# Pairs' products put first in each round of a fused DLRM kernel, gathers held behind them, and four table look-ups moved into the rounds

## The reference

```
e = stack([tbl_f[ids[:, f]] for f in range(32)], axis=1)    # 512 x 32 x 256
dots = einsum('bnd,bmd->bnm', e, e)
z = dots[:, i < j]                                          # 512 x 496
h = concatenate([z, dense_ctx], axis=1)                     # 512 x 512
h = maximum(h @ W_top1 + b_top1, 0)                         # 512 x 512
h = maximum(h @ W_top2 + b_top2, 0)                         # 512 x 256
y = h @ W_top3                                              # 512 x 1
```

## Time and profile before

| | |
|---|---|
| time, median of 3 runs | 162.37 us (161.98 to 162.54) |
| span of the profiled execution, first to last instruction | 231.2 us |
| the profiled execution's time beside its span | none is listed |
| TensorE busy, in the profiled execution | 178.4 us (77%) |
| GpSimd busy | 104.5 us (45%) |
| VectorE busy | 95.2 us (41%) |
| ScalarE busy | 77.3 us (33%) |
| mean granted TensorE clock | 0.874 |

### The profile page before, as it was taken

One profiled execution on the slowest core, in us unless ns is written; L12 is line 12 of the kernel. 1 busy time (PEld: TensorE's weight loads), 2 busy tenths in 40 slices (PEclk: granted clock), 3 DMA queues, 4 the chain that ended last, 5 costly groups with the idle time before them and its releaser, 6 DMA issues.

```text
span 231.2 us, 6208 instructions
## 1 busy us (share of the span) xinstructions
PE 178.4 (77%) x2678; PEld 151.4 (66%) x2678; DVE 95.2 (41%) x311; ACT 77.3 (33%) x190; POOL 104.5 (45%) x110
## 2 busy tenths in 40 slices
PE   7999952999958889868494394929559295999995
PEld 6688831688946778757392392819458184899774
DVE  2896310836902859753116014220603232534331
ACT  3376413746843244113032051400304032234232
POOL 2777775565874445372417336360723614300000
PEclk9999995599995999999889559785958769799999
DMA  5999653577883345541303213130220303100000
GB/s 154 311 371 311 172 145 104 171 259 207 256 299 117 122 154 151 184 114 29 91 3 101 80 27 98 41 113 3 71 68 26 106 11 94 45 6 4 4 6 0
DMA packets 12869, 26.77 MB, mean 116 GB/s; under 512 B 2917, under 2 KB 3881, under 8 KB 12842
## 3 DMA queue, kind: packets, MB, share of 16 engines
q0 software_dynamic: 4992, 13.64, 19.9%
q1 hardware_dynamic: 7706, 12.47, 16.5%
q10 hardware_dynamic: 144, 0.26, 0.5%
HBM read 26.36 MB, written 0.00 MB: 114 GB/s over the span
## 4 chain that ended last, share of the span: by engine, by line
PE 65%; issue 21%; ACT 9%; another core or an unknown queue 2%; DVE 1%; POOL 0%; POOLq 0%
PE bank L614 18%; PE bank L565 14%; PE bank L621 13%; PE xt_ps L584 11%; ACT high L450 3%; PE bank L648 3%; ACT kept L458 3%; PE bank L674 2%; ACT xt L463 2%; PE xt_ps L701 2%; PE xt_ps L674 1%; DVE pairs L394 1%; PE bank L682 1%; ACT h L496 0%
## 5 line engine op out<-in xcount | busy, mean ns | idle before, releaser
L346 POOL DMA_INDIRECT rows<-table,row_ids x104 | 103.8, 998 | 94.7 <-PE xt_ps L584 62.1
L614 PE MATMUL bank<-xt 128*32 128x32 f32 (+1 forms) x1664 | 45.2, 219 | 36.9 <-issue 36.0
L614 PEld LDWEIGHTS bank<-xt 128*32 128x32 f32 (+1 forms) x1664 | 35.0, 129 | 47.8 <-issue 44.1
L463 ACT COPY xt<-xt_ps 128x512 f32<-128x512 f32 (+1 forms) x43 | 22.2, 554 | 85.3 <-PE xt_ps L584 75.2
L394 DVE COPY pairs<-bank 32x64 f32<-32x64 f32 (+1 forms) x184 | 39.6, 215 | 12.7 <-PE bank L614 10.4
L377 DVE COPY xt<-xt_ps 128x512 f32<-128x512 f32 (+1 forms) x14 | 9.2, 654 | 84.8 <-PE xt_ps L584 84.8
L584 PE MATMUL xt_ps<-ident,rows 128*128 128x128 f32 x208 | 33.4, 306 | 7.1 <-issue 5.0
L565 PE MATMUL bank<-one_hot,high 128*128 128x512 f32 (+1 forms) x128 | 31.8, 369 | 2.2 <-issue 1.2
L621 PE MATMUL bank<-pairs,w_sb 128*128 128x128 f32 x192 | 32.2, 329 | 1.2 <-issue 1.2
L584 PEld LDWEIGHTS xt_ps<-ident,rows 128*128 128x128 f32 x208 | 26.7, 157 | 9.6 <-issue 5.9
L366 DVE TENSOR_SCALAR one_hot<-small_ids_sb,first_sb 128x512 fp32r<-128x512 int32 (+1 forms) x64 | 24.5, 422 | 17.4 <-remote 11.8
(11 more groups left out here) (36 smaller groups left out, 44.8 us busy)
## 6 DMA issues: line engine op xcount, KB each, us to landing
small_sb<-small_tables SPq DMA_DIRECT2D x31, 256.0 KB
w_sb<-w SPq DMA_DIRECT2D x8, 256.0 KB
rows<-table,row_ids POOLq DMA_INDIRECT x104
small_ids_sb<-small_ids SPq DMA_DIRECT2D x3, 256.0 KB
small_ids_sb<-small_ids SPq DMA_DIRECT2D x4, 128.0 KB
w_sb<-w SPq DMA_DIRECT2D x1, 512.0 KB, 5.6
small_ids_sb<-small_ids ACTq DMA_DIRECT2D x1, 256.0 KB
small_sb<-small_tables SPq DMA_DIRECT2D x2, 128.0 KB, 3.5
```

The source lines that it names most:

```text
L346: nc.gpsimd.indirect_dma_start(rows[:, i % ROWS, :], None, table, bass.IndirectOffsetOnAxis(ap=row_ids[:, i:i + 1], axis=0)).then_inc(gath ...
L463: nc.scalar.copy(*fill_parts(f)).then_inc(xt_act, 1)
L614: done = nc.tensor.matmul(dots_ps[later(n)][n % 2][quads, g, :], x, x, start=(c == 0), stop=(c == DC - 1))
```

## The change

- `AT_ONCE` is 2 for all batches, so a half is always 32 instructions of 64 columns.
- Ahead of the rounds stand twos 0 to 15 (tables 0 to 3) with 8 fills. Twos 16 to 31 (tables 4 to 7) are in rounds 0 to 5, as 2, 2, 2, 2, 4, 4. The fills of the rounds are 4, 3, 3, 3, 3, 4, 4, then 3 each, and 4 in round 14.
- In a round both halves come first, then layers 2 and 3, layer 1, the twos, and the fills.
- take_kept of batches 0 and 1 is behind two 15, and those of 2 to 7 are in rounds 0 to 3.
- A gather that reuses a row buffer waits for more than the transposes: gathers 14 to 20 for the end of two 9 (`chunk_used`), gathers from 21 on for a first half, `dots_half_done`: gathers 21 to 27 for that of batch 0, later ones for the first half of the round after the one in which the buffer was emptied.
- The eight parts of W_top1 and W_top2 are loaded between tables 5 and 6, once fills 7 to 10 (before: 16 to 23) are transposed.

```diff
-AT_ONCE = 2, 1
-FIRST_BATCHES = 6
+AT_ONCE = 2
...
-FILLS_BEHIND = {6: (0, 1, 2), 8: (3, 4, 5), 11: (6, 7, 8), 14: (9, 10, 11), 17: (12, 13), 21: (14, 15), 23: (16,)}
-EARLY = 17
-TWOS_AHEAD = 24
-TWOS_IN = [1, 1, 1, 1, 2, 1, 1]
-KEPT_BEHIND = {17: (0, 1), 20: (2, 3), 23: (4, 5)}
-KEPT_IN = {0: (6,), 1: (7,), 7: (8, 9), 8: (10, 11), 9: (12,), 10: (13,), 11: (14,), 12: (15,)}
-FILLS_IN = [2, 2, 1, 2, 3, 3, 4, 3, 3, 3, 3, 2, 2, 3, 4]
+FILLS_BEHIND = {6: (0, 1, 2), 9: (3, 4, 5), 12: (6, 7)}
+EARLY = 8
+PAUSE_BEHIND = 9
+FILLS_PAUSED = 4
+TWOS_AHEAD = 16
+TWOS_IN = [2, 2, 2, 2, 4, 4, 0]
+KEPT_BEHIND = {15: (0, 1)}
+KEPT_IN = {0: (2, 3), 1: (4, 5), 2: (6,), 3: (7,), 7: (8, 9), 8: (10, 11), 9: (12,), 10: (13,), 11: (14,), 12: (15,)}
+FILLS_IN = [4, 3, 3, 3, 3, 4, 4, 3, 3, 3, 3, 3, 3, 3, 4]
...
-FOUND_BANKS = [(2, 3), (0, 1)] * 3 + [(0, 1)] * 2
-PRODUCTS_FREE = 5
+FOUND_BANKS = [(2, 3), (0, 1)] * 2 + [(0, 1)] * 4
+PRODUCTS_FREE = 3
...
                 if fill_gathers(f)[-1] >= ROWS:
-                    pool.wait_ge(transposed, next(e for e in range(f) if fill_gathers(f)[-1] - ROWS in fill_gathers(e)) + 1)
+                    e = next(e for e in range(f) if fill_gathers(f)[-1] - ROWS in fill_gathers(e))
+                    pool.wait_ge(transposed, e + 1)
+                    if e < FILLS_PAUSED:
+                        pool.wait_ge(chunk_used, 2 * (PAUSE_BEHIND + 1))
+                    else:
+                        pool.wait_ge(dots_half_done, round_of(e) + 2 if e >= EARLY else 1)
...
-                if groups[-1] == GROUPS - 1:
-                    done.then_inc(dots_done, 1)
+                done.then_inc(dots_half_done if h == 0 else dots_done, 1)
...
             for r in range(ROUNDS):
+                dots(2 * r)
+                dots(2 * r + 1)
                 if r in LAYER2_IN:
                     layer2_of(LAYER2_IN[r])
                 if r in LAYER3_IN:
                     layer3(LAYER3_IN[r], l3_ps)
-                if r in LEAD_LAYER1:
-                    b, halves = LEAD_LAYER1[r]
+                if r in LAYER1_IN:
+                    b, halves = LAYER1_IN[r]
                     for i in halves:
                         layer1_half(b, i)
-                dots(2 * r)
-                if r in TRAIL_LAYER1:
-                    b, halves = TRAIL_LAYER1[r]
-                    for i in halves:
-                        layer1_half(b, i)
-                for two in twos_in(r)[:1]:
-                    look_up(two)
-                dots(2 * r + 1)
-                for two in twos_in(r)[1:]:
+                for two in twos_in(r):
                     look_up(two)
```

More of the change, by code:

```diff
@@ L51 @@
 TURNED_BY_ACT = 0, 1, 3
-FILLS_BEHIND = {6: (0, 1, 2), 8: (3, 4, 5), 11: (6, 7, 8), 14: (9, 10, 11), 17: (12, 13), 21: (14, 15), 23: (16,)}
-EARLY = 17
-TWOS_AHEAD = 24
-TWOS_IN = [1, 1, 1, 1, 2, 1, 1]
-KEPT_BEHIND = {17: (0, 1), 20: (2, 3), 23: (4, 5)}
-KEPT_IN = {0: (6,), 1: (7,), 7: (8, 9), 8: (10, 11), 9: (12,), 10: (13,), 11: (14,), 12: (15,)}
-FILLS_IN = [2, 2, 1, 2, 3, 3, 4, 3, 3, 3, 3, 2, 2, 3, 4]
+FILLS_BEHIND = {6: (0, 1, 2), 9: (3, 4, 5), 12: (6, 7)}
[7 more added lines that the diff above has]
+FILLS_IN = [4, 3, 3, 3, 3, 4, 4, 3, 3, 3, 3, 3, 3, 3, 4]
 ROUNDS = len(FILLS_IN)
[L67 to L70, removed]
+LAYER1_IN = {5: (0, [0, 1, 2]), 6: (0, [3, 4, 5]), 7: (0, [6, 7]), 9: (1, [0, 1, 2]), 10: (1, [3, 4, 5]),
+             11: (1, [6, 7]), 13: (2, [0, 1, 2, 3]), 14: (2, [4, 5, 6, 7])}
 RELU1_IN = {7: 0, 11: 1, 14: 2}
@@ L133, in build_tower @@
         banks = [ctx.enter_context(nc.psum_tensor(f"bank{n}", [P, 512], F32)) for n in range(5)]
-        dots_ps = [[bank[:, 0:GROUPS * n * Q].rearrange("p (g j) -> p g j", g=GROUPS) for bank in banks[2:4]]
-                   for n in AT_ONCE]
+        dots_ps = [bank[:, 0:GROUPS * AT_ONCE * Q].rearrange("p (g j) -> p g j", g=GROUPS) for bank in banks[2:4]]
         l1_ps = [[bank[:, n * BLOCK:(n + 1) * BLOCK] for n in range(N1)] for bank in (banks[4], banks[0])]
@@ L169, in build_tower @@
         kept_dve = sem("kept_dve")
+        dots_half_done = sem("dots_half_done")
         dots_done = sem("dots_done")
@@ L254, in fills_in, with round_of @@
             return range(EARLY + sum(FILLS_IN[:r]), EARLY + sum(FILLS_IN[:r + 1]))
-        def later(n):
-            return int(n >= FIRST_BATCHES)
+        def round_of(f):
+            return next(r for r in range(ROUNDS) if f in fills_in(r))
         def moves(n, s):
@@ L265, in moves @@
                 to = pairs[Q * q:Q * (q + 1), b % 2, skip:, at + s * GROUPS:at + (s + 1) * GROUPS]
-                column = s % AT_ONCE[later(n)] * Q + q * JJ
-                source = dots_ps[later(n)][n % 2][Q * s:Q * (s + 1), :, column + skip:column + JJ]
+                column = s % AT_ONCE * Q + q * JJ
+                source = dots_ps[n % 2][Q * s:Q * (s + 1), :, column + skip:column + JJ]
                 yield to, source.rearrange("i g j -> i j g")
@@ L318, in _ @@
                     load_dense(1)
[L319 to L323, removed]
+                if k == 5:
+                    for j in range(JJ):
+                        sp.wait_ge(transposed, EARLY + j // 2)
+                        sp.dma_start(w1_sb[:, j, :], w1[:, j, :]).then_inc(w1_in, 16)
+                    sp.dma_start(w2_sb[:], w2).then_inc(w2_in, 16)
             for b in range(2, NB):
@@ L606, in dots @@
                         pe.wait_ge(moved_dve, n - 1)
-                at_once = AT_ONCE[later(n)]
                 for g in groups:
                     for c in range(DC):
-                        for s in range(0, GROUP, at_once):
+                        for s in range(0, GROUP, AT_ONCE):
                             at = g * GROUP + s
-                            x = xt[:, n % KEEP, c, at:at + at_once, :].rearrange("d s f -> d (s f)")
-                            quads = slice(s * Q, (s + at_once) * Q)
-                            done = nc.tensor.matmul(dots_ps[later(n)][n % 2][quads, g, :], x, x,
+                            x = xt[:, n % KEEP, c, at:at + AT_ONCE, :].rearrange("d s f -> d (s f)")
+                            quads = slice(s * Q, (s + AT_ONCE) * Q)
+                            done = nc.tensor.matmul(dots_ps[n % 2][quads, g, :], x, x,
                                                     start=(c == 0), stop=(c == DC - 1))
-                if groups[-1] == GROUPS - 1:
-                    done.then_inc(dots_done, 1)
+                done.then_inc(dots_half_done if h == 0 else dots_done, 1)
             def layer1(b, n, columns, to):
```

## The result

| | before | after |
|---|---|---|
| time, median (4 runs each) | 162.45 us (161.98 to 162.85) | 180.93 us (180.37 to 181.12) |
| ratio | | 1.112, 95% interval 1.107 to 1.117 |
| span of the profiled execution | 231.2 us | 179.1 us |
| instructions | 6208 | 4977 |

A kernel's executions differ: some are a few per cent longer, at a lower granted clock, and the ratios leave these out while the medians hold them. The lists of the runs hold the span beside the time. The profiled execution after has 180.88 us beside 179.1, and the difference is 1.8 us in all of the lists: that is what lies around the span. So the two spans of the table must not be compared.

What follows compares the result with a forecast made beforehand. The gather stream was taken to set the end from round 8 on. `flip` moves from 137.35 to 150.4, 13.05 us, with 0.78 behind it 13.8; 162.4 + 13.8 = 176.2 us, range 167 to 184.

Steps and rivals of the forecast that it cites:

- Rival C: TensorE is the bound, gathers come closer than 1.25 us, 15.5 us lie around the span: 182.6 us, chance 0.14.
- The gaps as the profiler's doing: Before's profiled execution: 48 us of TensorE issue gaps and the low clock come from profiling, so timed runs lack them.
- Around the span: Time outside before's span: the rebuilt end at 156.3 leaves 6.1 us to the timed median.
- The first hold: Ahead of batch 0: TensorE idles 2.6 us, gather 21 starts at 42.3 instead of 34.1, the stream 8.2 us late.
- Halves: Twenty halves become 64-column: 7.8 us more TensorE work, 0.78 in round 14 and 0.78 in batch 15 on the path.
- Twos in the rounds: Rounds 3 and 4: VectorE's preparations delay fills 18 and 21; TensorE waits 2.8 us in round 3, round 4 repeats it.
- The second hold: Gather 56 waits for dots(12)'s first half, ending at 88.4, against 86.05 by its own pace: 2.4 us.
- W1 comes earlier: Tables 6 and 7 load behind W1's 2.5 MB: zero, or a microsecond or two of round 4.
- B: The first hold alone counts, VectorE's queue is shorter and copies hide: 172.2 us, chance 0.20.
- E: In between, the stream makes up its 8 us through shorter pauses: 163 to 168 us, chance 0.09.
- D: Not slower: gaps before 32-column products are partly real in timed runs and the change removes them; 160.3, chance 0.07.
- A: The likeliest case, the summed terms with the gather stream setting the end: 176.2 us, chance 0.50.

Runs made afterwards that it cites:

- E6: Before with 64-column halves for all batches and gather 56 held until the products of batch 6: 172.23 us, ratio to before 1.061.
- E1: Before with 64-column halves for all batches, nothing else changed: 162.80 us, ratio to before 1.0087.
- E10: E1 with take_kept of batches 0 to 3 behind twos 20 and 22 instead of 17 and 20: 163.67 us, ratio to before 1.0065.
- E11: Before, 32-column halves kept, with take_kept of batches 0 to 3 behind twos 20 and 22 instead of 17 and 20: 164.01 us, ratio to before 1.0071.
- E4: After with 32-column halves from batch 6 on: 185.01 us from four executions of 181.23 to 187.38, too uneven for a ratio.
- E8: After with the added waits of gathers 14 to 27 only, later ones waiting for transposes alone: 175.99 us, ratio to before 1.087.
- E5: E1 with both halves first in each round, layers and twos behind them: 164.39 us, ratio to before 1.017.
- E9: E2 with fills 15, 18 and 21 copied by ScalarE instead of VectorE: 170.83 us, ratio to before 1.044.
- E3: After with W_top1 and W_top2 loaded behind tables 6 and 7: 177.28 us, ratio to before 1.091.
- E12: E2 with W_top1 and W_top2 loaded behind tables 6 and 7, as in E3: 172.53 us, ratio to before 1.062.
- E2: After without the added waits of the gathers, which wait for the transposes alone: 172.04 us, ratio to before 1.065.
- E7: After with the added waits of gathers from 28 on only, 14 to 27 waiting for transposes alone: 175.42 us, ratio to before 1.084.

## Why the prediction was right, point by point

**What bounds the kernel.** Right: the gather stream, at 1.25 us a gather. Shown by E6 (a pause is paid in full), by E1 (7.8 us more of TensorE's work cost 1.4) and E10 (1.4 us won ahead of the rounds were gone at once); E11's chain agrees. Rival C is excluded by E6 and E1, and by the 1.8 us around the span where it needed 15.5. The margin is thinner than forecast: TensorE's own `flip` was put 9.5 us ahead of the gathers' in before, and in E1, with 7.0 us more of halves ahead of it, the two are 1 us apart. In after the last gather that held TensorE was gather 91, as the sum had it, landed at 142.15 instead of 134.2.

**The gaps as the profiler's doing.** This step fell. E11's profiled execution has 6208 instructions and no such gaps, and one of E11's ten timed executions took 232 us, like the profiled one of before. So the long execution is a rare kind, and tracing alone doesn't make it. For the sum it made no difference, since the clean spacings were used. What sets it off isn't known; it was seen only with 6208 instructions, once in E11's ten and in none of 54 timed executions of before. Shorter gaps of its kind stand in E4's trace.

**Around the span.** Mis-sized: 6.1 us, measured 1.8. The rebuilt span of before, 156.3, was thus some 4 us short of 160.6. One part is the landing of a gather, taken as 2.0, with a median of 3.2 after and 3.1 in E1; another is the stream, which was 1.6 us later at gather 97 (130.71 in E1, forecast 129.1), as single gathers ahead of gather 56 took up to 1.63 us on GpSimd. Both stand on either side and drop out of the difference.

**The first hold.** Right almost to the figure: batch 0 at 41.2 predicted, 41.42 measured; the wait of TensorE 2.6, measured 2.61; gather 21 at 42.3, measured 44.12. Of the 1.8 us too little 0.9 are the low clock of the first half (1.94 us, priced 1.08), 0.8 lie between the end of the half, 43.36, and the start of the gather, which were priced at nothing. E8: the first hold alone costs 3.6 us by the ratios, 6.0 by the spans.

**Halves.** Right in before's order: 7.8 us of work, 1.56 on the path; E1 measured 0.9%, 1.4 us. In after's order the small halves didn't win it back (E4). The Trainium skill, "TensorE: Matmul & The Clock Gate", section "Wait — 56ns, not 53.3ns?", has a floor of about 25 ns between small products; by that figure, an estimate, E1 would have saved some 10 us of TensorE's work. The measurement disagrees: E1 is not faster, and E11's trace has halves of 64 products in 0.69 us again (119.23 to 119.92), 10.8 ns apart.

**Products first.** Right: after's halves waited for ScalarE's copy 11 times, 7.8 us in all, 0.7 each. What it costs in the end is 1 us or so (E5).

**Twos in the rounds.** Right in mechanism and nearly in size: fills 18 and 21 were copied behind the preparations and held batches 4 and 5. Predicted waits 2.8 (its own figures, 66.6 less 64.1, make it 2.5) and 0.8, measured 3.21 and 1.37. What it is worth for the end is argued, not shown: E9 took the fills away and the wait moved to ScalarE.

**The second hold.** Right in place, gather 56 to the number, and mis-sized: predicted at 88.4, measured 95.39. The pause of 1.81 us ahead of gather 51 was not forecast. The 7.0 us are TensorE's lateness in rounds 0 to 5. 1.55 is the slow clock of batch 0, 3.95 waits for gathers in round 1 (0.29, 2.59, 1.07), 1.5 the slow clock of batch 2 behind them: 7.0 together. The other differences cancel. The slow clock was not in the sum, and the late rows were priced at zero: **"W1 comes earlier ... zero, or if the cover fails a microsecond or two of round 4"** is the term that failed. It failed in round 1, not 4, since the 2.5 MB lengthened the landing of the gathers that the first hold had just let go: with late W1 (E3) that wait is 1.25 us, with early W1 3.95, 3.61 (E8) and 4.12 (E4). What it is worth in the end is less sure, 3.3 us by E3's ratio with the clock's part unknown. E12 shows that it needs the hold: without holds, late W1 brings nothing.

**The sum.** Added: 13.8 us on 162.4; measured 18.5. By the ratios to before 1.4 us are the halves (E1), 1.4 the order (E5 less E1), 7.7 the plan of fills, twos and W1 (E2 less E5) and 7.6 the holds (after less E2), each known to 1 us or so; the sum is 18.1. The spans of single executions give 0.8, 6.6 and 10.8 for the last three. The sum had the direction and the chain of causes; that it came out 4.7 us short is the waits of round 1 and the low clock. (Its `flip` of 150.4 adds up to 150.3.)

**The rivals.** B had one hold only; E7 and E8 show two with equal shares. C fell by E6 and E1, and E (163 to 168) is missed by far. D, no: nothing was faster. But gaps of its kind are real in E4, and there after with small halves is not faster than after, rather slower. A was the case, beyond its own range of 174 to 179, within the stated one.

## What to carry to other kernels

Where one engine issues a long series at a fixed pace and its last item has a fixed tail behind it, a wait laid on that series is paid in full as long as the series sets the end (E6), however well it fits the other engines' work, and in part where another engine is as late (E7, E8); look up the pace, multiply, and compare with the span before anything else. Price a load that is moved against every transfer in flight at its new place, those above all that another edit has just made urgent. Compare kernels by several executions of each, and a trace by where it stands among them: here single spans made the holds 10.8 us where the ratios say 7.6. And check that the profiled execution is a usual one (its span beside the timed median) before a gap in it is treated as the thing to remove.

## What the runs showed of the hardware

- The granted clock fell behind an idle stretch of TensorE of 2.61 us in some executions and not in others: after batch 0's wait the two halves took 3.63 us in after (clock 0.57 from 41 to 45 us), 3.62 in E7, 3.60 in E8 and 3.53 in E12, and 2.08 in E2, E3, E4 and E9, each behind the same 2.61 us.
- 128x32 products ran 10.8 ns apart, as pairs of loads and products (64 in 0.69 us), at the full clock.
- In after the landing of one gather of 128 rows went from 2.7 to 8.2 us, median 3.2. The one issued at 50.75 took 7.5, and from 53 to 59 us 351 GB/s were moved.
- Most indirect gathers cost GpSimd 0.94 or 0.95 us and 0.30 to the next, in every kernel; single ones, while VectorE prepared twos, up to 1.89 (E2, at 50.52). From gather 56 to 103 it was 58.77 to 59.16 us in thirteen kernels.
